# One memset instead of two between paced gathers, and 124 gathers instead of 120 ahead of the first scatter

## The reference, cut to what matters

```
h = maximum(layernorm(x), 0)
row, col = src, dst
deg = segment_sum(ones, row, n);  deg_inv = where(deg > 0, rsqrt(maximum(deg, 1)), 0)
norm = deg_inv[row] * deg_inv[col]
msg[e] = sum_b comps[type[e], b] * (h[col[e]] @ bases[b]) * alpha[type[e]] * norm[e]
return x + segment_sum(msg, row, n)
```

## Time and profile before

| | |
|---|---|
| time, median of 3 runs | 722.61 us (721.76 to 723.48) |
| profiled execution | 723.03 us, span 721.2 us |
| busy share of the span | DVE 82%, PE 78%, POOL 78%, PE weight loads 55%, ACT 51% |
| memsets of line 358 | 128, mean 165 ns |
| gathers of line 368 | 196, mean 1155 ns |
| scatters of line 389 | 196, mean 1598 ns, first at 218.1 us, last at 712.8 us |
| moved by DMA | 108.88 MB |

### The profile page before, as it was taken

One profiled execution on the slowest core, in us unless ns is written; L12 is line 12 of the kernel. 1 busy time (PEld: TensorE's weight loads), 2 busy tenths in 40 slices (PEclk: granted clock), 3 DMA queues, 4 the chain that ended last, 5 costly groups with the idle time before them and its releaser, 6 DMA issues.

```text
span 721.2 us, 13608 instructions
## 1 busy us (share of the span) xinstructions
PE 562.8 (78%) x3922; PEld 399.7 (55%) x3922; DVE 593.3 (82%) x2624; ACT 364.7 (51%) x1494; POOL 562.7 (78%) x532
## 2 busy tenths in 40 slices
PE   4999996666667888567799879977888888889940
PEld 3766665444455665345566656655666566655620
DVE  7999999468768798656999999989999989997820
ACT  0345354545444888335556545664555565546620
POOL 3888888777778878878788878877888878776885
PEclk9999999789897999877999999999999999999975
DMA  8899999989984546344544554454545545444332
GB/s 278 274 344 322 348 324 325 344 294 315 312 297 68 97 85 121 52 77 65 110 69 88 91 107 84 86 96 91 85 96 96 99 80 98 80 60 85 33 34 25
DMA packets 56573, 108.88 MB, mean 151 GB/s; under 512 B 9339, under 2 KB 48264, under 8 KB 55684
## 3 DMA queue, kind: packets, MB, share of 16 engines
q0 software_dynamic: 34496, 25.72, 26.9%
q1 hardware_dynamic: 4688, 50.95, 19.1%
q10 hardware_dynamic: 17316, 31.36, 14.2%
HBM read 94.89 MB, written 64.61 MB: 221 GB/s over the span
## 4 chain that ended last, share of the span: by engine, by line
DVE 45%; PE 21%; issue 10%; DMA 9%; ACT 7%; POOL 7%; ACTq 1%; SPq 0%; POOLq 0%; DVEq 0%
DVE masked L477 9%; PE pst L737 8%; DVE part_sum L514 8%; PE pst L756 8%; DVE turned_hot L471 6%; DVE rows L454 6%; POOL out_dram L389 6%; DVE same L533 4%; DVE rows L455 4%; DVE rows L514 4%; DMA out_dram<-rows,scatter_idx 3%; DMA edge_row<-edge_rows 2%; ACT part_sum L646 2%; PE pst L764 2%; PE pst L766 2%
## 5 line engine op out<-in xcount | busy, mean ns | idle before, releaser
L389 POOL DMA_INDIRECT out_dram<-rows,scatter_idx x196 | 313.2, 1598 | 78.3 <-issue 46.4
L368 POOL DMA_INDIRECT rows<-in_x_dram,dst_i x196 | 226.4, 1155 | 68.9 <-issue 27.7
L737 PE MATMUL pst<-table_bits,turned_hot 128*128 128x198 f16 x1568 | 176.1, 260 | 72.1 <-DVE masked L477 53.5
L756 PE MATMUL pst<-bases_sb,h_turned 128*128 128x512 f32 x392 | 212.8, 626 | 0.0
L737 PEld LDWEIGHTS pst<-table_bits,turned_hot 128*128 128x128 f16 x1568 | 141.9, 102 | 100.1 <-issue 50.2
L514 DVE SCALAR_TENSOR_TENSOR part_sum<-pst,coef,part_sum 128x128 f32<-128x128 f32 x392 | 115.6, 344 | 77.3 <-ACT part_sum L646 65.3
L646 ACT ACTIVATE part_sum<-pst,coef 128x128 f32<-128x128 f32 x196 | 71.1, 363 | 167.1 <-PE pst L756 129.1
L764 PEld LDWEIGHTS pst<-rows,same 128*128 128x128 f32 x392 | 72.3, 196 | 149.0 <-issue 121.6
L477 DVE SCALAR_TENSOR_TENSOR masked<-iota_h,lo,pst 128x198 f32<-128x198 f16 x392 | 141.8, 416 | 10.9 <-PE pst L737 7.9
L764 PE MATMUL pst<-rows,same 128*128 128x128 f32 x392 | 81.0, 289 | 43.1 <-ACT rows L653 38.3
L591 ACT ACTIVATE scratch<-rows 128x128 f32<-128x128 f32 x196 | 57.9, 299 | 73.1 <-DMA rows<-in_x_dram,dst_i 72.7
(11 more groups left out here) (72 smaller groups left out, 438.5 us busy)
## 6 DMA issues: line engine op xcount, KB each, us to landing
out_dram<-in_x_dram SPq DMA_DIRECT2D x46, 1000.0 KB
src_row<-src_rows ACTq DMA_DIRECT2D x25, 512.0 KB
edge_row<-edge_rows ACTq DMA_DIRECT2D x44, 256.0 KB
out_dram<-in_x_dram ACTq DMA_DIRECT2D x4, 1000.0 KB
rows<-in_x_dram,dst_i POOLq DMA_INDIRECT x196
out_dram<-rows,scatter_idx POOLq DMA_INDIRECT x196
rows<-edge_rows ACTq DMA_DIRECT2D x10, 175.0 KB
edge_row<-edge_rows SPq DMA_DIRECT2D x5, 256.0 KB
```

Of the source, the lines that this page charges most:

```text
L368: pool.indirect_dma_start(row(t), None, x, bass.IndirectOffsetOnAxis(ap=dst_i[:, t:t + 1], axis=0)) \
L389: pool.indirect_dma_start(out, bass.IndirectOffsetOnAxis(ap=scatter_idx[:, t:t + 1], axis=0), row(t), None, compute_op=ALU.add) \
L737: last = pe.matmul(pst[:, LOOK + t % 2, k * LO:(k + 1) * LO], turned_hot[:, g % 2, c, k * W + j * P:k * W + (j + 1) * P], table[:, c * LO: ...
L756: pe.matmul(pst[:, PRODUCT + t % 4, :], h_turned[:, g % 2, j, :], bases_sb[:].rearrange("d b f -> d (b f)"), start=True, stop=True).then_i ...
```

## The change

Between two gathers of the stretch from the end of the histogram to the first scatter stands one memset with its wait, where there were two, and this stretch has 68 gathers, where it had 64. The gathers of the scatter loop are 72 instead of 76. Through `gathers_until` the new constant also enters `stats_until`, and so ACT's order.

```diff
-    HIST_GATHERS, FIRST_GATHERS = 56, 120
+    HIST_GATHERS, FIRST_GATHERS = 56, 124
...
                 elif HIST_GATHERS <= t < FIRST_GATHERS:
-                    for _ in range(2):
-                        beats[0] += 1
-                        pool.memset(beat[:], 0.0).then_inc(beat_ended, 1)
-                        pool.wait_ge(beat_ended, beats[0])
+                    beats[0] += 1
+                    pool.memset(beat[:], 0.0).then_inc(beat_ended, 1)
+                    pool.wait_ge(beat_ended, beats[0])
```

## The result

The changed kernel took 781.69 us (median of four executions, 775.8 to 790.38) against 722.63 us before (four executions, 721.76 to 723.48). The ratio is 1.079, with a 95% interval of 1.0744 to 1.0834. It is 59 us slower, where I had forecast 2.2 us faster. Medians here are of all executions; ratios leave out those that are over 1.5% above the fastest of their kernel, so the two can differ a little. The profiled execution took 782.13 us, with a span of 780.2 us.

The account below looks back on a forecast made before the run. Up to 325 us the end was taken to follow the first scatter, set by POOL's paced gathers with the copies close behind. First scatter -2.2 us, other terms nothing: 722.61 to 720.4 us, range 717.5 to 723.5.

Parts of the forecast that it names:

- edge-row loads: Sign of error: loads compute awaited in 112 to 218 us come late enough to use up its 9.12 us wait.
- the rivals: Three alternatives: gain hidden behind the copies (0.28), more gain than forecast (0.13), interval not shortening, so slower (0.09).
- Rival (c): Paced gathers: interval stays 1.656 because gathers stretch, first scatter 224.8, time 729.3 us; chance 0.09, with a lost compute lead.
- The interval: Paced gathers, 112 to 218 us: one memset less takes 0.17 us, interval from 1.656 to 1.486.
- the figure by group in the prediction: Paced gathers: alternative estimate of one memset's cost, (21.1 + 3.7) / 128 = 0.19 us.
- The copies: Before the first scatter: six more gathers delay the copies' landing 1.5 us to 215.5; scatter at 215.9, 2.2 us earlier.
- the lower bound: Before the first scatter: gathers fit into gaps, copies do not move, scatter at 214.4, a gain of 3.7 us.
- 0.26 us per gather: Paced stretch: time of all 16 DMA engines per gather, from q0's 15.5% of 94 us over 57 gathers.
- First scatter to the end: From the first scatter on: its shift of -2.2 us is carried whole to the end, microsecond for microsecond.
- Four gathers fewer later: Scatter loop: four gathers vanish, 5.5 us of POOL in all, but compute sets the pace there; costed at nothing.
- ScalarE's order: Row statistics from step 9 on, read one group further; longer lead eaten, both long waits keep their scatter slots; nothing.

Follow-up runs that it names:

- e5: The kernel before with no memset between the paced gathers, 120 gathers ahead, on chip 5: 717.81 us, ratio 0.995.
- c2: e5 again, unaltered, on chip 11: 793.21 us, ratio 1.097.
- d2: e5 with gathers of 64 rows instead of 128 for tiles 56 to 114, on chip 5: 720.58 us, ratio 0.995.
- e7: The kernel before (120 gathers ahead) with one memset of 190 words instead of two of 40, on chip 5: 720.57 us, ratio 0.995.
- d1: e5 again, unaltered, on chip 5, as control for d2: 721.09 us, ratio 0.995.
- e3: The changed kernel with its one memset 270 words wide instead of 40, on chip 7: 729.59 us, ratio 1.012.
- e2: The changed kernel's 124 gathers ahead, but two memsets of 40 words as in the kernel before, on chip 7: 729.45 us, ratio 1.011.
- c4: e7 again, unaltered, on chip 11: 724.86 us, ratio 1.002.
- e6: The changed kernel with its one memset 120 words wide instead of 40, on chip 5: 720.97 us, ratio 0.998.
- e1: The changed kernel with 120 gathers ahead instead of 124, so only the memset removed, on chip 7: 779.47 us, ratio 1.082.
- e4: The changed kernel with only 24 of its 50 row copies, on chip 7: 776.75 us, ratio 1.076.
- e11: The changed kernel with a four-word memset without semaphore increment or wait, on chip 0: 792.28 us, ratio 1.093.
- e12: e5 with 124 gathers ahead instead of 120, no memset, on chip 0: 796.53 us, ratio 1.102.
- c3: e6 again, unaltered, on chip 11: 764.69 us, executions too far apart for a ratio.

## Why the prediction was wrong

**The step that failed** is one that I never priced as a step: that compute between 112 and 218 us goes on as before, whatever the gathers' pace. The prediction followed POOL's time into the copies and into the first scatter, and put no term for compute into the sum; it stood only among the signs of being wrong, as edge-row loads that would have to come 9% of that stretch later. In fact compute nearly stopped, and its first finished tile came 72.8 us late. None of the rivals had it. Rival (c) ended on the right side and its words "with a lost lead of compute" stood in the list of chances, but its mechanism was a gather that stretches; the gathers took 962 ns on average, less than the 987 of the earlier trace rows.

**The interval.** Forecast 1.486 as a mean, measured 1.42. Nearly half of the gap of 0.06 is the memset: a pair lasts 0.34 us and one alone 0.15, so taking one away was worth 0.19 to 0.20 (1.57 to 1.37 in the plain case), as the figure by group in the prediction had it, and not 0.17. The rest is that slow gathers were rarer. Those seem to come with a busy VectorE (on average 992 ns in e5, where compute ran, and 964 in c2, the same program, where it stood), so their going is a sign of the hold-up rather than a gain.

**The copies.** Forecast later by 1.5 us, at 215.5. In the changed kernel q1's last packet falls in 200 to 202 instead of 213.5 to 214, since ACT's queue carried 272 packets over 112 to 206 where it had carried 2048: a held-up compute asks for no edge rows. Where compute ran on, q1's last packet fell in 215.5 to 216 (d2), 214.5 to 215 (e5 and e7), 213.5 to 214 (d1), 213 to 213.5 (e3), 211 to 211.5 (e2), 210 to 211 (c4) and 209 to 210 (e6), and the three kernels with 124 gathers ahead are not the late ones. The end of the copies moves by 6 us between executions for reasons that I did not find, and the gathers moved ahead cannot be seen in it. My 1.5 us was too much, and the lower bound (the copies do not move) nearer. That the first scatter came at 215.88 in e5 and 216.14 in e7, where 215.9 was forecast, is luck with this spread. The prediction also set its 0.26 us per gather against the Trainium skill's 0.95 us as if they were one quantity; 0.26 is a share of the time of all 16 engines and 0.95 the length of one transfer, so the rows do not contradict it.

**First scatter to the end.** Right where compute keeps its lead: e2 lost 6.1 us at the first scatter and 7.5 at the end, and in e6's profiled execution the first scatter is 3.8 us earlier and the last one 4.4 (708.44 against 712.8). By the medians e6 is only 1.9 us faster, so what of it reaches the end is not resolved. Not applicable in the changed kernel, where POOL waits for compute.

**Four gathers fewer later, ScalarE's order.** Forecast at nothing. e1 and the changed kernel differ only in these and lie 2 us apart, within the spread of either, so there is nothing against it. ScalarE's two long waits stay bound to the scatters as forecast: in e6 they end at 301.38 and 323.06, 3.5 us earlier than in the earlier trace rows, behind a first scatter 3.8 us earlier.

**What is shown and what isn't.** Shown: the loss is the shorter spacing of the gathers (e1, e2, e3); the copies' load on the DMA engines, the memset, its signals and the four gathers ahead are not needed for it (e4, e11, e12, c2); it acts through what TensorE announces to VectorE and ScalarE, whose signals are raised late; it is there on three chips and not on chip 5 (e5 and d1 against c2; e6 against c3). Open: why that signal is late, and whether the matmul's write or only the signal is; whether it is POOL's writing of descriptors or the gathers' transfers that does it; whether the gathers are too many or their rows; what differs between chips; and whether the changed kernel itself would be held up on chip 5, where it wasn't run. The Trainium skill (SBUF — State Buffer, the section on SBUF's two separate sides) states that a compute instruction can't be slowed by a DMA, nor TensorE wait on any other for its access. The runs do not contradict this for the memory's ports, since VectorE's pick took 0.42 us in both kernels; TensorE's own durations are modelled and can't tell. But whoever reads the rule as "gathers can't delay TensorE's chain" is refuted by e4: 31.4 us of such waits with hardly any other DMA on the core.

No kernel tried is a safe gain over the one before. The quickest, e5, wins 0.5% on chip 5 and loses 9.7% on chip 11. e7, with one memset of 190 words, wins as much on chip 5, and on chip 11 (c4) its interval of 0.998 to 1.0065 takes in 1.

## What to carry to other kernels

An instruction that only spaces a queue can be load-bearing for engines that have nothing to do with that queue: before shortening it, count as a rival that what it spaces disturbs somebody else, and look in the first trace for signals that come late. The view of waits of the kernel before shows no wait without a releaser in the paced stretch; only the recorded times of the signals did, with transposes that ended at 169.99 and were signalled at 171.19. When an engine's consumer starts many microseconds after its producer's recorded end, pair the two off by hand over the whole stretch, since the groups by line name no cause for it. And a kernel this near to such an edge must be timed on several chips, since one chip's verdict (0.995) and another's (1.097) can both be right.

## What the runs showed of the hardware that was not expected

- With indirect gathers of 128 rows issued every 1.26 to 1.44 us, TensorE's results reached VectorE and ScalarE up to 24 us late in the changed kernel (43 us in c2), while signals from VectorE to TensorE arrived in 0.06 us. At 1.51 us the latest was 3.3 us late (c4), at 1.57 us 1.2 us (the kernel before), and on chip 5 none was late at any interval down to 1.22.
- It needs no other DMA traffic to speak of (e4: share of the gathers 15.5%, all else about 1%).
- With no memset between the gathers it lasted 11 us beyond the last one (e12: last gather issued at 198.8, signals at 209.95 and 210.04, nothing busy on the core from 200.4), with one 1 to 3 us.
- POOL took 0.91 us to issue a gather of 64 rows (d2) and 0.95 us for one of 128 (e5).
- The same program differed by 75 us between two chips (717.81 and 793.21), while the kernel before took 722.89 and 723.44 on them.
